# Attention scores: one VectorE instruction that masks, scales, moves and keeps the extreme, in place of mask matmuls, a reduction and a scaling

## The chip, the cores and the metric

One Trainium2 chip, one of its cores. The metric is the device time of one launch in microseconds. Before the change it was measured in three runs, with a median of 2131.19 us (2128.11 to 2140.74).

## What is computed

A sequence of two transformer-like layers on x of shape 2 x 1024 x 256 in float32: a Mamba-2 block with a gated MLP, a feed-forward block with weights from a lookup table, causal attention, and a mixture of experts. The change is in the attention alone:

```
q = einsum('bpd,hde->bphe', x, W_Q) + b_Q        # k and v in the same way
scores = einsum('bqhe,bkhe->bhqk', q, k) / sqrt(128)
scores = where(tril(ones((S, S))), scores, -100000.0)
attn = softmax(scores, axis=-1)
z = einsum('bkhe,bhqk->bqhe', v, attn)
out = einsum('bqhe,hed->bqd', z, W_O) + b_O      # S = 1024, 16 heads of 128, batch 2
```

## The kernel before

Matrix products of float32 precision are made of three passes over pairs (hi, lo): a value rounded to the matrix engine's fast float type and the rest. Every tensor that enters a product is therefore made twice: ACT writes hi from PSUM, DVE writes lo as the difference (L1597 to L1599 and L1642 to L1645).

Attention goes over 2 batches, and in each over 8 pairs of heads. An order of events is written out by hand in `section`, and each engine runs through the same list and picks its own part (`handle`). There are three kinds of section. "first" makes q, k and v of pair 0 and then the scores of its head 0 with nothing between them. "body" runs in a hardware loop, 7 turns per batch: it turns and sums the probabilities of one pair while it makes the scores of the next, the projections of the next pair, and the output of this one. "last" is a body without a next pair; it has the following norm in it.

A score tile t has 128 queries and (t+1) x 128 keys (t from 0 to 7), in two PSUM banks; tiles take turns with two such places. For a tile:

1. PE makes three passes for each chunk of up to 512 keys (L1525, L1529, L1530). In the chunk that ends on the diagonal it adds the causal mask with one more matmul, of a bf16 mask by a bf16 identity (L1528). Before it starts it waits until the exponential of tile t-2 is done (L1519), which frees the place.
2. DVE takes the negated maximum of the row (L1648), drains, and multiplies it by the scale (L1650).
3. ACT makes the exponential from PSUM into SBUF with that bias, and the row's sum (L1604; a second instruction reads the sum).
4. DVE takes the reciprocal of the sum (L1653), GpSimd multiplies the probabilities by it in place (L1692).
5. PE turns 128 x 128 blocks of the probabilities (L1538), ACT and DVE make the pair pt_hi, pt_lo of them, and PE sums with v (L1551 to L1559). The work banks 4 to 6 take turns; a sum waits for its own pt_lo, which is asked for two chunks ahead.
6. After the last chunk of a group ACT gathers z (L1612, L1614), DVE makes its lo (L1657), and PE multiplies it by W_O; DVE adds the output to x (L1661).

DVE's order in a chunk is: reciprocal of the tile before, maximum of this tile, pt_lo. ACT's is: pt_hi, gather, exponential, projection.

Of the kernel before, what the change touches and what calls it, by code (L numbers as in the profile page):

```python
# [7 lines left out]
BF16 = mybir.dt.bfloat16  # L8
# [6 lines left out]
P = 128  # L15
# [1231 lines left out]
def attention_stage(nc, sems, mem, s, a, before, norm):  # L1247
# [10 lines left out]
    def sb(what, shape, dt=F32):  # L1258
        return mem.enter_context(nc.sbuf_tensor(f"attn_{what}", shape, dt))
# [3 lines left out]

    q, k, v = pair("q", [P, 2, SEQ]), pair("k", [P, 2, SEQ]), pair("v", [P, QT, 2 * AE])
    z, pt = pair("z", [P, 2, SEQ]), pair("pt", [P, 3, GROUP])
    probs = [[sb(f"probs_{h}_{g}", [P, TG, (g + 1) * GROUP]) for g in range(2)] for h in range(2)]
    qkv_raw, wo_raw = sb("qkv_raw", [P, 3, KD, 2, AE]), sb("wo_raw", [P, 2, D])
    qkv, wo = pair("qkv", [P, 3, KD, 2, AE]), pair("wo", [P, 2, D])
    z_raw = sb("z_raw", [P, GROUP])
    bias = sb("bias", [P, 3, AH])  # L1270
    b_out = sb("b_out", [P, D])
    ident_b, mask = sb("ident_b", [P, P], BF16), sb("mask", [P, P], BF16)
    neg_max, sums, inverse = (sb(n, [P, 2 * QT]) for n in ("neg_max", "sums", "inverse"))

    small_loaded, qkv_loaded, wo_loaded, masks_ready = (
# [129 lines left out]
    def first_column(e):  # L1405

        return max(0, e["j"] - TG * e["g"]) * P

    def score_view(e):
        width = (e["t"] + 1) * P  # L1410
        slot = 2 * (e["t"] % 2)
        return s.psum[:, slot:slot + 2, :].rearrange("p b c -> p (b c)")[:, 0:width]

    def probs_view(e):
        return probs[e["h"]][e["t"] // TG][:, e["t"] % TG, 0:(e["t"] + 1) * P]

    def stat(tensor, e):
        at = e["h"] * QT + e["t"]
# [60 lines left out]

    def tensor(pe):  # L1480
        pe.wait_ge(*before)
        pe.wait_ge(masks_ready, 4)
        pe.sem_inc(summed, 3)

        def handle(e, counts, b, kind, i):
            what = e["what"]
            if what == "norm" and e["step"] == "turn":

                pe.wait_ge(exp_done, counts.at("tile", QT))
                norm["turn"](pe, norm_group(e, b))  # L1490
            if what in ("project", "values"):

# [21 lines left out]
            elif what == "score":  # L1514
# [1 line left out]
                pe.wait_ge(work_done, counts.at("work", e["need"]))  # L1516

                ahead = max(0, e["tile"] - 1) if kind == "first" else e["tile"] - 1
                pe.wait_ge(exp_done, counts.at("tile", ahead))  # L1519
                t, view = e["t"], score_view(e)  # L1520
                queries = pair_at(q, slice(None), e["h"], slice(t * P, (t + 1) * P))
                for at in range(0, (t + 1) * P, GROUP):
                    end = min(at + GROUP, (t + 1) * P)
                    (q_hi, q_lo), (k_hi, k_lo) = queries, pair_at(k, slice(None), e["h"], slice(at, end))
                    pe.matmul(view[:, at:end], q_hi, k_hi, start=True, stop=False)  # L1525
                    if end == (t + 1) * P:

                        pe.matmul(view[:, t * P:], ident_b[:, :], mask[:, :], start=False, stop=False)  # L1528
                    pe.matmul(view[:, at:end], q_hi, k_lo, start=False, stop=False)  # L1529
                    last = pe.matmul(view[:, at:end], q_lo, k_hi, start=False, stop=True)  # L1530
                last.then_inc(scores_ready, 1)
            elif what == "turn":

                tile = TG * (e["g"] + 1)
                ready = counts.at("tile", tile - QT) if e["h"] == 0 else counts.at("tile", tile)
                pe.wait_ge(probs_ready, ready)
                for lq in range(first_column(e) // P, TG):
                    last = pe.transpose(s.psum[:, work_bank(e), lq * P:(lq + 1) * P],  # L1538
                                        probs[e["h"]][e["g"]][:, lq, e["j"] * P:(e["j"] + 1) * P], s.ident[:, :])
                last.then_inc(work_ready, 1)  # L1540
            elif what == "sum":

                pe.wait_ge(work_done, counts.at("work", e["work"] + 1))
                j = e["j"]
                if j == 0:

                    pe.wait_ge(z_read, 1 + counts.at("z", 2 * e["h"] + e["g"]))
                at = first_column(e)
                v_hi, v_lo = pair_at(v, slice(None), j, slice(e["h"] * AE, (e["h"] + 1) * AE))
                p_hi, p_lo = pair_at(pt, slice(None), e["pt"] % 3)  # L1550
                pe.matmul(s.psum[:, 7, at:], v_hi, p_hi[:, at:], start=j == 0, stop=False, skip_group_check=True)  # L1551
                pe.matmul(s.psum[:, 7, at:], v_hi, p_lo[:, at:], start=False, stop=False, skip_group_check=True)  # L1552

                ends = at + P if j >= TG * e["g"] else at
                if ends > at:
                    last = pe.matmul(s.psum[:, 7, at:ends], v_lo, p_hi[:, at:ends], start=False, stop=True,
                                     skip_group_check=True)
                if ends < GROUP:
                    last = pe.matmul(s.psum[:, 7, ends:], v_lo, p_hi[:, ends:], start=False, stop=False, skip_group_check=True)  # L1559
                last.then_inc(summed, 1)  # L1560
            elif what == "output":

                pe.wait_ge(z_done, 1 + counts.at("z", 4))
                pe.wait_ge(w_split, counts.at("w", 1 if kind == "last" else 4))
                for t in range(2):
                    tokens = slice((2 * e["t"] + t) * P, (2 * e["t"] + t + 1) * P)
                    for h in range(2):
                        last = three_passes(pe, s.psum[:, work_bank(e), t * D:(t + 1) * D],
                                            pair_at(z, slice(None), h, tokens), pair_at(wo, slice(None), h), h == 0, h == 1)
                last.then_inc(work_ready, 1)  # L1570
# [3 lines left out]
    def scalar(act):  # L1574
# [4 lines left out]
        def handle(e, counts, b, kind, i):  # L1579
# [21 lines left out]
                norm["high"](act, norm_group(e, b))  # L1601
            elif what == "exp":
                act.wait_ge(max_ready, counts.at("tile", e["tile"] + 1))
                act.activation(probs_view(e), score_view(e), ACT.Exp, bias=stat(neg_max, e), scale=SCORE_SCALE,  # L1604
                               accum_out=stat(sums, e)).then_inc(exp_done, 1)
            elif what == "gather":

# [14 lines left out]
    def vector(dve):  # L1622
# [9 lines left out]
            dve.drain()  # L1632

        add_bias(0)

        def handle(e, counts, b, kind, i):
            what = e["what"]
# [7 lines left out]
                    dve.tensor_tensor(lo, work_view(e), hi.bitcast(F32), ALU.subtract).then_inc(work_done, 1)  # L1645
            elif what == "score":
                dve.wait_ge(scores_ready, counts.at("tile", e["tile"] + 1))
                dve.tensor_reduce(stat(neg_max, e), score_view(e), AX_X, ALU.max, negate=True)  # L1648
                dve.drain()
                dve.tensor_scalar(stat(neg_max, e), stat(neg_max, e), SCORE_SCALE, None, ALU.mult).then_inc(max_ready, 1)  # L1650
            elif what == "invert":
                dve.wait_ge(exp_done, counts.at("tile", e["tile"] + 1))
                dve.reciprocal(stat(inverse, e), stat(sums, e)).then_inc(inverse_ready, 1)  # L1653
# [16 lines left out]
    def gpsimd(pool):  # L1670

        pool.wait_ge(*before)
        pool.memset(ident_b[:, :], 0.0).then_inc(masks_ready, 1)
        pool.memset(mask[:, :], 0.0).then_inc(masks_ready, 1)
        pool.wait_ge(masks_ready, 2)
        pool.affine_select(out=ident_b[:, :], in_=ident_b[:, :], compare_op=ALU.not_equal, fill=1.0, base=0,
                           pattern=[[-1, P]], channel_multiplier=1).then_inc(masks_ready, 1)
        pool.affine_select(out=mask[:, :], in_=mask[:, :], compare_op=ALU.is_ge, fill=MASKED, base=0,
                           pattern=[[-1, P]], channel_multiplier=1).then_inc(masks_ready, 1)

        def handle(e, counts, b, kind, i):
# [652 lines left out]
```

## Time and profile before

| | us |
|---|---|
| median of 3 runs | 2131.19 |
| the profiled execution, its own time | 2131.62 |
| its span, first to last instruction | 2129.9 |
| attention, first to last of its matmuls | 718 to 1783 |

The profile is of one execution. A row of a group of instructions gives the line, engine, operation, output<-inputs, shapes and count, then the busy time in us and the mean of one in ns, then the engine's idle time before them and what ended it. A matmul's row is longer than the time by which it delays the next, since matmuls overlap: for PE the distance from start to start is the price. "granted clock" is the share of TensorE's full speed.

### The profile page before, as it was taken

Reading aid. Unit: us, or ns where it says so; the run is one execution under the profiler, and the core shown is the slowest. Engines: PE = TensorE matmul, PEld = TensorE weight load, DVE = VectorE, ACT = ScalarE, POOL = GpSimd, SP = SyncE. Lnnn points to the kernel's source line nnn. Section 1 sums busy time; section 2 is a strip of 40 time slices with the busy share of each in tenths; the row PEclk is TensorE's granted clock in tenths of the full one; section 3 lists DMA queues with packets and bytes.
Section 4 is the critical chain, followed back from the end, with each engine's and each line's share of the span. In section 5 each row is a group of like instructions: output and inputs, shape, how many; then the busy total and the mean of one; then the engine's idle time right before and its main releaser. Section 6 shows DMA issues by size and latency. Waiting matters only on the chain.

```text
span 2129.9 us, 34088 instructions
## 1 busy us (share of the span) xinstructions
PE 1897.3 (89%) x10870; PEld 1542.8 (72%) x10870; DVE 1400.8 (66%) x2757; ACT 972.2 (46%) x1984; POOL 638.8 (30%) x634
## 2 busy tenths in 40 slices
PE   2699889888999799999999989999999996999997
PEld 1455555577788578888888877888888885788886
DVE  6656362388865466666666656666666666688887
ACT  2333233255533265555655536555565553233332
POOL 5123234333333132222222213222222221234342
PEclk9789989799999899999999989999999998899999
DMA  3000001100000200000000000000000001000001
GB/s 95 1 1 1 1 1 40 50 15 12 5 1 1 39 21 20 20 20 0 20 20 5 16 20 21 20 20 19 1 20 20 5 1 45 16 16 30 15 0 40
DMA packets 59807, 37.71 MB, mean 18 GB/s; under 512 B 16488, under 2 KB 56656, under 8 KB 59728
## 3 DMA queue, kind: packets, MB, share of 16 engines
q1 hardware_dynamic: 59728, 36.71, 6.0%
q8 instruction: 44, 0.72, 0.1%
q14 instruction: 35, 0.29, 0.0%
HBM read 34.60 MB, written 2.10 MB: 17 GB/s over the span
## 4 chain that ended last, share of the span: by engine, by line
PE 71%; DVE 15%; ACT 5%; issue 4%; DVEq 3%; POOL 1%; DMA 0%; SPq 0%; ACTq 0%; POOLq 0%
PE psum L52 12%; PE psum L54 12%; PE psum L53 12%; PE psum L1538 6%; PE psum L1529 3%; PE psum L1525 3%; PE psum L1551 3%; PE psum L1530 3%; PE psum L1552 3%; PE psum L1559 3%; DVE mamba_conv_sum L1075 3%; PE psum L951 2%; PE psum L953 2%; DVE table_leaves L561 2%; ACT attn_probs L1604 1%
## 5 line engine op out<-in xcount | busy, mean ns | idle before, releaser
L1692 POOL TENSOR_SCALAR attn_probs<-attn_probs,attn_inverse 128x128 f32<-128x128 f32 (+7 forms) x256 | 191.0, 747 | 614.3 <-DVE attn_inverse L1653 614.1
L1599 ACT ACTIVATE attn_pt_hi<-psum 128x512 fp32r<-128x512 f32 (+3 forms) x384 | 185.6, 488 | 236.2 <-PE psum L1538 234.0
L1645 DVE TENSOR_TENSOR attn_pt_lo<-psum,attn_pt_hi 128x512 fp32r<-128x512 f32 (+3 forms) x384 | 211.4, 555 | 61.4 <-ACT attn_pt_hi L1599 58.0
L1604 ACT ACTIVATE attn_probs<-psum,attn_neg_max 128x128 f32<-128x128 f32 (+7 forms) x256 | 188.8, 737 | 118.8 <-DVE attn_neg_max L1650 118.4
L1538 PE MATMUL psum<-ident,attn_probs 128*128 128x128 f32 x1152 | 190.2, 276 | 27.7 <-DVE x_tok L1661 11.9
L1648 DVE TENSOR_REDUCE attn_neg_max<-psum 128x1 f32<-128x128 f32 (+7 forms) x256 | 192.0, 750 | 17.8 <-PE psum L1530 14.3
L1551 PE MATMUL psum<-attn_pt_hi,attn_v_hi 128*128 128x512 f32 (+3 forms) x384 | 162.3, 423 | 23.2 <-DVE attn_pt_lo L1645 17.6
L1538 PEld LDWEIGHTS psum<-ident,attn_probs 128*128 128x128 f32 x1152 | 137.6, 141 | 49.6 <-DVE attn_pt_lo L1645 18.6
L1529 PE MATMUL psum<-attn_k_lo,attn_q_hi 128*128 128x512 f32 (+3 forms) x384 | 151.9, 395 | 0.0
L1968 POOL TENSOR_TENSOR moe_hid_lo<-moe_hidden,moe_hid_hi 128x512 fp32r<-128x512 f32 x64 | 82.9, 1296 | 199.2 <-ACT moe_hid_hi L1941 199.2
L1525 PE MATMUL psum<-attn_k_hi,attn_q_hi 128*128 128x512 f32 (+3 forms) x384 | 136.7, 356 | 5.7 <-ACT attn_probs L1604 5.0
L1552 PE MATMUL psum<-attn_pt_lo,attn_v_hi 128*128 128x512 f32 (+3 forms) x384 | 134.8, 351 | 0.0
L1530 PE MATMUL psum<-attn_k_hi,attn_q_lo 128*128 128x512 f32 (+3 forms) x384 | 133.9, 349 | 0.0
L395 POOL TENSOR_TENSOR gated_h_lo<-gated_hidden,gated_h_hi 128x512 fp32r<-128x512 f32 x56 | 78.4, 1399 | 176.4 <-ACT gated_h_hi L383 176.4
L52 PE MATMUL psum<-act_hi,moe_gu_hi 128*128 128x512 f32 x256 | 105.9, 414 | 16.3 <-DVE moe_up L2041 13.1
L52 PE MATMUL psum<-act_hi,attn_qkv_hi 128*128 128x512 f32 x256 | 105.4, 412 | 15.8 <-POOL attn_qkv_lo L1685 15.8
L1559 PE MATMUL psum<-attn_pt_hi,attn_v_lo 128*128 128x512 f32 (+3 forms) x320 | 116.6, 364 | 0.0
L1685 POOL TENSOR_TENSOR attn_qkv_lo<-attn_qkv_raw,attn_qkv_hi 128x512 fp32r<-128x512 f32 x48 | 60.8, 1284 | 152.4 <-ACT attn_qkv_hi L1589 152.4
L53 PE MATMUL psum<-act_lo,moe_gu_hi 128*128 128x512 f32 x256 | 104.6, 409 | 0.0
L54 PE MATMUL psum<-act_hi,moe_gu_lo 128*128 128x512 f32 x256 | 104.2, 407 | 0.0
L54 PE MATMUL psum<-act_hi,attn_qkv_lo 128*128 128x512 f32 x256 | 103.0, 402 | 0.0
L53 PE MATMUL psum<-act_lo,attn_qkv_hi 128*128 128x512 f32 x256 | 102.4, 400 | 0.0
(322 smaller groups left out, 5479.2 us busy)
## 6 DMA issues: line engine op xcount, KB each, us to landing
attn_qkv_raw<-in_L_attn_W_Q_dram SPq DMA_DIRECT2D x32, 128.0 KB, 2.2
attn_qkv_raw<-in_L_attn_W_K_dram SPq DMA_DIRECT2D x32, 128.0 KB, 2.4
attn_qkv_raw<-in_L_attn_W_V_dram SPq DMA_DIRECT2D x32, 128.0 KB, 2.5
attn_wo_raw<-in_L_attn_W_O_dram SPq DMA_DIRECT2D x16, 256.0 KB, 3.0
moe_gu_raw<-_L_ffn_gate_up_proj_dram SPq DMA_DIRECT2D x8, 512.0 KB, 3.8
x_in<-_attn_hidden_states_dram SPq DMA_DIRECT2D x4, 512.0 KB, 5.6
x_tok<-_attn_hidden_states_dram SPq DMA_DIRECT2D x4, 512.0 KB, 5.9
moe_down_raw<-in_L_ffn_down_proj_dram SPq DMA_DIRECT2D x8, 256.0 KB, 4.1
```

The costliest lines, as they stand in the source:

```text
L52: pe.matmul(out, s_hi, m_hi, start=start, stop=False)
L53: pe.matmul(out, s_hi, m_lo, start=False, stop=False)
L54: return pe.matmul(out, s_lo, m_hi, start=False, stop=stop)
L1525: pe.matmul(view[:, at:end], q_hi, k_hi, start=True, stop=False)
L1529: pe.matmul(view[:, at:end], q_hi, k_lo, start=False, stop=False)
L1530: last = pe.matmul(view[:, at:end], q_lo, k_hi, start=False, stop=True)
L1538: last = pe.transpose(s.psum[:, work_bank(e), lq * P:(lq + 1) * P], probs[e["h"]][e["g"]][:, lq, e["j"] * P:(e["j"] + 1) * P], s.ident[:, :])
L1551: pe.matmul(s.psum[:, 7, at:], v_hi, p_hi[:, at:], start=j == 0, stop=False, skip_group_check=True)
L1552: pe.matmul(s.psum[:, 7, at:], v_hi, p_lo[:, at:], start=False, stop=False, skip_group_check=True)
L1604: act.activation(probs_view(e), score_view(e), ACT.Exp, bias=stat(neg_max, e), scale=SCORE_SCALE, accum_out=stat(sums, e)).then_inc(exp_do ...
L1645: dve.tensor_tensor(lo, work_view(e), hi.bitcast(F32), ALU.subtract).then_inc(work_done, 1)
L1648: dve.tensor_reduce(stat(neg_max, e), score_view(e), AX_X, ALU.max, negate=True)
```

## The change

The two bf16 constants and the mask matmul go. The mask becomes a float32 tile of 128 x 1024, zero but for its last 128 columns, whose part above the diagonal is -1e30. For each tile one DVE instruction (`tensor_tensor_reduce` with add and min) reads the scores from PSUM and the last (t+1) x 128 columns of the mask from SBUF, adds them, multiplies by minus the scale, writes the result to the probabilities' tile in SBUF, and keeps its minimum, which is the negated scaled maximum. The reduction, the drain and the scaling go. ACT's exponential reads and writes that SBUF tile in place, with scale -1. PE's scores, and the norm's transposes that use the same banks, wait for `max_ready` instead of `exp_done`. The probabilities of a head lie packed, row after row, where they were a rectangle for each half.

```
-    probs = [[sb(f"probs_{h}_{g}", [P, TG, (g + 1) * GROUP]) for g in range(2)] for h in range(2)]
+    probs = [sb(f"probs_{h}", [P, QT * (QT + 1) // 2 * P]) for h in range(2)]
-    ident_b, mask = sb("ident_b", [P, P], BF16), sb("mask", [P, P], BF16)
+    mask = sb("mask", [P, SEQ])
+    def row_start(t):
+        return t * (t + 1) // 2 * P
     def probs_view(e):
-        return probs[e["h"]][e["t"] // TG][:, e["t"] % TG, 0:(e["t"] + 1) * P]
+        return probs[e["h"]][:, row_start(e["t"]):row_start(e["t"] + 1)]
+    def probs_block(e, t):
+        at = row_start(t) + e["j"] * P
+        return probs[e["h"]][:, at:at + P]
...
     def tensor(pe):
-        pe.wait_ge(masks_ready, 4)
...
-                pe.wait_ge(exp_done, counts.at("tile", QT))
+                pe.wait_ge(max_ready, counts.at("tile", QT))
                 norm["turn"](pe, norm_group(e, b))
...
-                pe.wait_ge(exp_done, counts.at("tile", ahead))
+                pe.wait_ge(max_ready, counts.at("tile", ahead))
...
                     pe.matmul(view[:, at:end], q_hi, k_hi, start=True, stop=False)
-                    if end == (t + 1) * P:
-                        pe.matmul(view[:, t * P:], ident_b[:, :], mask[:, :], start=False, stop=False)
...
-                                        probs[e["h"]][e["g"]][:, lq, e["j"] * P:(e["j"] + 1) * P], s.ident[:, :])
+                                        probs_block(e, TG * e["g"] + lq), s.ident[:, :])
...
             elif what == "exp":
-                act.activation(probs_view(e), score_view(e), ACT.Exp, bias=stat(neg_max, e), scale=SCORE_SCALE,
+                act.activation(probs_view(e), probs_view(e), ACT.Exp, bias=stat(neg_max, e), scale=-1.0,
                                accum_out=stat(sums, e)).then_inc(exp_done, 1)
...
         add_bias(0)
+        dve.wait_ge(masks_ready, 2)
...
                 dve.wait_ge(scores_ready, counts.at("tile", e["tile"] + 1))
-                dve.tensor_reduce(stat(neg_max, e), score_view(e), AX_X, ALU.max, negate=True)
-                dve.drain()
-                dve.tensor_scalar(stat(neg_max, e), stat(neg_max, e), SCORE_SCALE, None, ALU.mult).then_inc(max_ready, 1)
+                dve.sem_inc(s.wait_over, 1)
+                dve.tensor_tensor_reduce(probs_view(e), score_view(e), mask[:, (QT - 1 - e["t"]) * P:], -SCORE_SCALE, -MASKED,
+                                         ALU.add, ALU.min, stat(neg_max, e)).then_inc(max_ready, 1)
...
     def gpsimd(pool):
-        pool.memset(ident_b[:, :], 0.0).then_inc(masks_ready, 1)
         pool.memset(mask[:, :], 0.0).then_inc(masks_ready, 1)
-        pool.wait_ge(masks_ready, 2)
-        pool.affine_select(out=ident_b[:, :], in_=ident_b[:, :], compare_op=ALU.not_equal, fill=1.0, base=0,
-                           pattern=[[-1, P]], channel_multiplier=1).then_inc(masks_ready, 1)
-        pool.affine_select(out=mask[:, :], in_=mask[:, :], compare_op=ALU.is_ge, fill=MASKED, base=0,
+        pool.wait_ge(masks_ready, 1)
+        pool.affine_select(out=mask[:, SEQ - P:], in_=mask[:, SEQ - P:], compare_op=ALU.is_ge, fill=MASKED, base=0,
                            pattern=[[-1, P]], channel_multiplier=1).then_inc(masks_ready, 1)
```

## Rows read from the trace of the kernel before

**Rows 1.** The page's head: span, and busy us (share) xinstructions of each engine.

```profile
span 2129.9 us, 34088 instructions
...
PE 1897.3 (89%) x10870; PEld 1542.8 (72%) x10870; DVE 1400.8 (66%) x2757; ACT 972.2 (46%) x1984; POOL 638.8 (30%) x634
```

**Rows 2.** Windows: stretch and length, busy us of each engine, granted clock, DMA.

```profile
737.60:754.40 16.80, 11.83 (x60) 8.12 (x59) 9.53 (x28) 8.60 (x21) 5.79 (x8) 0.90 0.00 0
...
880.50:943.80 63.30, 60.49 (x388) 52.21 (x388) 41.80 (x92) 37.55 (x80) 16.95 (x20) 1.00 0.06 17
```

**Rows 3.** Waits of PE in attention: us in total, times, longest us.

```profile
PE psum L1551 <- DVE attn_pt_lo L1645: 17.6, 21, 2.4
...
PE psum L1538 <- DVE x_tok L1661: 11.9, 14, 0.9
PE psum L1538 <- DVE attn_pt_lo L1645: 11.6, 13, 0.9
...
PE psum L1525 <- ACT attn_probs L1604: 5.0, 5, 1.5
```

**Rows 4.** Groups by line and shape.

```profile
L1528 PE MATMUL psum<-attn_mask,attn_ident_b 128*128 128x128 bf16 x256 | 59.4, 232 | 0.0
...
L1648 DVE TENSOR_REDUCE attn_neg_max<-psum 128x1 f32<-128x1024 f32 x32 | 38.9, 1215 | 0.6 <-PE psum L1530 0.6
...
L1648 DVE TENSOR_REDUCE attn_neg_max<-psum 128x1 f32<-128x128 f32 x32 | 9.1, 286 | 0.0
...
L1103 DVE TENSOR_TENSOR mamba_mixed<-mamba_decay,psum 128x1024 f32<-128x1024 f32 x16 | 19.5, 1222 | 14.1 <-ACT mamba_decay L1018 11.5 <-issue 2.6
...
L561 DVE COPY_PREDICATED table_leaves<-table_bits,table_leaves 128x512 f32<-128x512 uint8 x49 | 45.2, 954 | 3.2 <-issue 0.5
...
L1614 ACT ACTIVATE attn_z_hi<-attn_z_raw 128x512 fp32r<-128x512 f32 x64 | 40.5, 632 | 2.0
...
L1599 ACT ACTIVATE attn_pt_hi<-psum 128x512 fp32r<-128x512 f32 x192 | 114.5, 596 | 158.7 <-PE psum L1538 156.6
```

**Rows 5.** Timeline of PE in a body turn: start us, us, engine, line.

```profile
904.08 0.39 PE L1525 MATMUL psum<-attn_k_hi,attn_q_hi 128*128 128x512 f32 x1
...
904.76 0.39 PE L1525 MATMUL psum<-attn_k_hi,attn_q_hi 128*128 128x512 f32 x1
...
905.58 0.49 PE L1538 MATMUL psum<-ident,attn_probs 128*128 128x128 f32 x3
905.82 0.31 PE L1551 MATMUL psum<-attn_pt_hi,attn_v_hi 128*128 128x128 f32 x1
...
906.19 0.27 PE L1525 MATMUL psum<-attn_k_hi,attn_q_hi 128*128 128x128 f32 x1
...
906.60 0.41 PE L1538 MATMUL psum<-ident,attn_probs 128*128 128x128 f32 x2
```

**Rows 6.** Timeline of the same turn, the chain to PE's wait at 910.74.

```profile
907.21 0.15 DVE L1650 TENSOR_SCALAR attn_neg_max<-attn_neg_max 128x1 f32<-128x1 f32 x1
...
907.82 1.10 ACT L1604 ACTIVATE attn_probs<-psum,attn_neg_max 128x1024 f32<-128x1024 f32 x1
...
909.13 0.29 DVE L1648 TENSOR_REDUCE attn_neg_max<-psum 128x1 f32<-128x128 f32 x1
...
909.69 0.37 ACT L1604 ACTIVATE attn_probs<-psum,attn_neg_max 128x128 f32<-128x128 f32 x1 [0.41 <-DVE attn_neg_max L1650]
...
910.74 0.63 PE L1538 MATMUL psum<-ident,attn_probs 128*128 128x128 f32 x4 [0.94 <-DVE attn_pt_lo L1645]
```

**Rows 7.** Timeline of the first section of batch 0.

```profile
739.10 0.28 DVE L1648 TENSOR_REDUCE attn_neg_max<-psum 128x1 f32<-128x128 f32 x1
...
751.85 1.11 ACT L1604 ACTIVATE attn_probs<-psum,attn_neg_max 128x1024 f32<-128x1024 f32 x1 [0.79 <-DVE attn_neg_max L1650]
...
754.39 0.77 PE L1551 MATMUL psum<-attn_pt_hi,attn_v_hi 128*128 128x512 f32 x1 [2.42 <-DVE attn_pt_lo L1645]
```

**Rows 8.** Timeline of POOL at attention's start.

```profile
716.94 3.72 POOL L1685 TENSOR_TENSOR attn_qkv_lo<-attn_qkv_raw,attn_qkv_hi 128x512 fp32r<-128x512 f32 x3 [10.33 <-ACT attn_qkv_hi L1589]
```

## The prediction

> **What bounds the kernel now.** I read the busy shares first [rows 1]: the matrix engine is busy for 89% of the span, the vector engine for 66%, the activation engine for 46%. Such a mean hides stages, so next came the stages of attention alone [rows 2]. Attention runs from 718 to 1783 us. It holds two "first" sections (the row of 737.6 to 754.4 is the scores of one), fourteen body turns (seven per batch; the row of 880.5 to 943.8 is one, 63.3 us long) and two "last" sections. In a body turn PE is busy for 60.49 of 63.30 us at a granted clock of 1.00, with DVE at 41.80 and ACT at 37.55. So a body turn ends when PE has issued its stream: what leaves PE's stream is gained, what leaves DVE or ACT is gained only where PE waits for them. In a first section PE is busy for only 11.8 of 16.8 us; there nothing is interleaved with the scores, and the round trip PE, DVE, ACT sets the time.
>
> Third, what PE waits for in attention [rows 3]. The wait of L1538 for x_tok (14 times, 0.85 us) is an output tile and is untouched. The wait of L1538 for attn_pt_lo (13 times, 0.9 us) is one per body turn; its chain is in [rows 6]. The wait of L1525 for attn_probs (5.0 us in 5) is the scores waiting for the exponential of the tile two before, and lies in the first sections. The longest wait for attn_pt_lo, 2.4 us, stands at the end of a first section [rows 7].
>
> **The change part by part.**
>
> *Mask matmuls gone from PE (256).* The row of L1528 says 232 ns each, 59.4 us in all [rows 4], but matmuls overlap, so starts are what counts [rows 5]. Three passes over 512 columns without a mask matmul start at 904.08 and the next at 904.76: 0.68 us. The same three with one in between go from 904.76 to 905.58: 0.82 us. The mask costs 0.14, with width 512. At width 128, three passes of a sum without mask take 905.82 to 906.19, 0.37 us; scores with mask take 906.19 to 906.60, 0.41: only 0.04, since narrow passes wait for weights anyway. For widths 256 and 384 I have no clean pair here and take 0.13, near the 512 case. The last chunk of the eight tiles of a head has width 128 twice and a wider one six times: 2 x 0.04 + 6 x 0.13 = 0.86 us a head, 1.72 us a body turn. Not all of it shows: two 128-wide tiles and one 256-wide one lie just ahead of a wait that DVE or ACT ends (such as the one that ends at 910.74 [rows 6]); there PE would only wait longer. That leaves 1.72 - 0.08 - 0.13 = 1.51 us a turn, times 14 = 21.1 us. Bounds: 0.07 a mask on the exposed 13 (13 us in all), and 1.72 on each turn (24 us).
>
> *One fused DVE instruction for reduce, drain and 1-element scaling.* Before: 1215 ns at 1024 elements, 286 at 128, mean 750 [rows 4], then 0.15 us of L1650; at 909.13 the reduce begins and at 909.69 the exponential [rows 6]. The fused form is not in the trace. It reads PSUM and SBUF and writes SBUF, as L1103 does: 1222 ns at 1024. So streaming the scores out costs nothing over reducing them. The extreme has to be read out: a small instruction such as L1650 costs about 0.15 us [rows 6], of which I take half, 0.08, as seen. Taken: reduce's time plus 0.08, a saving of about 0.1 a tile. Bounds: below, the reduce alone (0.2 saved); above, the slowest two-input row, L561 at 954 ns for 512, 1.38 times a tensor_tensor of that width, plus a full 0.15: 1.8 us at 1024, 0.4 more than today's pair. In the body DVE has 21 us to spare a turn, so this matters only on the chain of [rows 6].
> The Trainium skill, VectorE: DVE Perf Modes, section "Two Vector instructions with no wait between them", says that an operation that also writes out its accumulator is two instructions; by it the read-out would have a row of its own, and the gain a tile would be near nothing. No run shown here tells.
>
> *The exponential reads SBUF instead of PSUM.* ACT's copy of 512 takes 632 ns from SBUF (L1614) and 596 from PSUM (L1599) [rows 4]: 0.04 us more, 256 times, 9 us of ACT, hidden under PE except twice on the chain of each turn.
> The Trainium skill on the same page, section "The TRN2 errata", gives 224 against 172 cycles, which would be an estimated 0.043 us; the rows agree.
>
> *The chain per body turn* [rows 6]: exponential of tile 7 (held up by the gather ahead of it on ACT, not by its maximum), its reciprocal, the maximum of tile 0, its exponential, pt_hi, pt_lo, PE at 910.74. New: -0.13 for the fused maximum (0.56 becomes 0.43), +0.04 for each of two exponentials: 0.05 less a turn. I count 0; bounds -2 and +3 us over 14 turns.
>
> *Score slots free earlier.* The scores of tile t wait for the maximum of t-2, not its exponential. In the body this wait hardly exists. In a first section it is the rhythm [rows 7]: the first reduce starts at 739.10, the exponential of tile 7 at 751.85, PE goes on at 754.39 after it. New: eight fused instructions, 8 x 0.75 + 8 x 0.08 = 6.6 us; seven reciprocals between them at 0.1, since DVE's order is maximum t, reciprocal t-1; and 0.6 in which DVE waits for scores of a still narrow tile: 7.9 us, last exponential at 747.1, 4.75 us sooner. PE needs twice 0.68 = 1.36 us for tile 7 without its mask [rows 5], about DVE's time, so it keeps up at full clock; but the clock granted in that stretch is 0.90 [rows 2], and I take off 0.75 for matmuls at the lower level. So 4.0 a section (2 to 5.5), 8 for both. Behind it the same order follows: what was late, PE's wait for pt_lo of chunk 0, stays and moves forward.
>
> *The last sections* hold eight scores each: 0.86 less 0.1 covered, 1.5 us for both (0 to 3).
>
> *Costed at nothing:* packed probabilities (same elements, all rows contiguous; transposes read 128-column blocks as before); PE's removed wait for the masks; DVE's new one, long met; GpSimd's mask of 1024 floats, made in the 10.33 us in which POOL waits for the first weights [rows 8]; if that cover were gone it would cost, once, less than the 3.72 us of the three subtractions of 512 behind it. DVE now writes the SBUF tile where ACT did, and nothing new is queued behind a wait.
>
> **Sum.** 21.1 + 0 + 8 + 1.5 = 30.6 us off the profiled execution's 2131.62 (its span is 2129.9): 2101. That execution lies 0.4 us above the median of 2131.19.
>
> **Rivals.**
> 1. *The fused instruction is slow per element*, two steps of 1.04 ns each instead of one (mean 576 elements: 0.6 us more). For it: no row shows the form. Against it: every two-input row at 512 lies between 689 and 954 ns. The body's slack takes most of it, since a sum waits for a pt_lo made two chunks earlier; but the maximum of tile 7 is 1.07 longer less the 0.15 of L1650, of which only the 0.46 from 907.36 to 907.82 are slack [rows 6], so the chain starts 0.46 late, and tile 0's is 0.13 longer: 0.59 x 14 = 8.3. A first section gains nothing (4.0 - 4.8). Sum: -21.1 + 8.3 + 1.6 - 1.5 = -12.7, 2119: within 1%.
> The Trainium skill, Vector Engine (DVE) Microarchitecture Reference, section "Points that are easy to get wrong", has a form of accumulating instruction halve its rate with two SBUF sources that are not bf16; here one source is PSUM, so by its words it would not apply, and nothing shown here tests it.
> 2. *Only the matmuls count*: the first sections stay, because PE runs them at the lower clock or the fused instruction lands at its upper bound. 2131.6 - 21.1 - 1 = 2110, the border of 1%.
> 3. *Slower: a fixed cost of the fused instruction*, x us whatever the width. It enters the chain of [rows 6] twice (once less about 0.5 of slack) and eight times in each first section: 14 x (2x - 0.5) + 16x = 44x - 7. It cancels the 30.6 at x = 0.85 us; at x = 1.3 the time is 2151. L1650's 0.15 us for one element speaks against it.
> 4. *More gained*: full clock in the first sections and the upper bound of the matmuls: 24 + 11 + 3 + 2 = 40, 2092.
>
> **How the numbers follow.** 1% of 2131, about what a measurement of this kernel can tell from no change, is 21 us: faster means under 2110. Chances: my forecast (2095 to 2108) 0.56, rival 4 0.10, rival 2 0.14 (half on each side of the border), rival 1 0.12, rival 3 0.08. Faster: 0.56 + 0.10 + 0.07 = 0.73; within 1%: 0.07 + 0.12 + 0.01 = 0.20; slower 0.07. The range goes from rival 4's 2092 to 2114, past rival 2; outside it lie rivals 1 and 3.
>
> **What would show it.** No L1528 rows, and body turns of 61.8 us instead of 63.3. Fused rows of about 1.22 to 1.3 us at 1024 and 0.29 to 0.37 at 128. First sections of 13 us. PE's L1525 waiting for DVE, briefly. The same two 0.86 us waits of PE a turn. It is wrong if the turn keeps 63 us (other waits took the mask's time), if the fused row at 1024 is over 2 us, or if PE waits for attn_pt_lo more than once or twice a turn.

## The result, and the profile after

| | before | after |
|---|---|---|
| median, us | 2135.41 (4 runs, 2128.11 to 2140.74) | 2103.19 (4 runs, 2100.11 to 2105.40) |
| profiled execution, us (its span) | 2131.62 (2129.9) | 2105.28 (2103.6) |

The ratio of the medians is 0.985, with a 95% interval from 0.982 to 0.988: 1.5% faster, 32 us by the medians and 26 us by the two profiled executions. The forecast was 2101, with the range 2092 to 2114.

The stages, marked in both traces by the same matmuls of PE (us):

| stage | before | after |
|---|---|---|
| first section, batch 0 / batch 1 | 16.73 / 16.64 | 12.83 / 12.83 |
| seven body turns, batch 0 / batch 1 | 442.45 / 444.87 | 432.04 / 431.98 |
| a typical body turn | 63.27 | 61.83 |
| last section up to its last score, batch 0 | 19.91 | 19.10 |
| rest of it, batch 0 | 34.81 | 36.89 |
| last section, batch 1 | 51.47 | 50.67 |
| everything ahead of attention's first projection | 718.35 | 722.24 |

First sections -7.7, body turns -23.3, last sections +0.5, the part ahead of attention +3.9, and +0.3 in the projections ahead of a batch's first scores and after attention: -26.3 together. The +3.9 isn't the change's: with the same code there, the kernels below have 717.4 to 721.9. Of the -23.3, 14 x 1.44 = 20.2 is the typical turn. The rest is the clock: four of before's fourteen turns hold a stretch at half speed, and two of after's (the first of each batch). Such a stretch makes a turn about 1.5 us longer, as two neighbouring turns of before show:

```profile
1475.80:1540.60 64.80, 62.12 (x390) 53.60 (x390) 41.86 (x92) 37.73 (x80) 16.96 (x20) 0.97 0.06 16
1540.60:1603.80 63.20, 60.52 (x390) 52.22 (x390) 41.81 (x92) 37.62 (x80) 16.96 (x20) 1.00 0.05 17
```

(stretch, length, busy us of PE, weight load, DVE, ACT, POOL, granted clock, DMA.)

The page's head of after, as [rows 1]:

```profile
span 2103.6 us, 33574 instructions
...
PE 1860.5 (88%) x10614; PEld 1537.1 (73%) x10614; DVE 1363.8 (65%) x2757; ACT 979.4 (47%) x1984; POOL 639.7 (30%) x632
```

Windows of after, as [rows 2] and with the same columns: the first section, a body turn (the fourth of batch 0, where [rows 2] has the third; they are alike), the rest of the last section of batch 0.

```profile
741.80:754.70 12.90, 8.85 (x51) 7.07 (x49) 8.48 (x28) 8.83 (x21) 5.84 (x8) 1.00 0.00 1
...
939.50:1001.30 61.80, 58.52 (x372) 52.10 (x372) 39.40 (x92) 38.03 (x80) 16.98 (x20) 1.00 0.06 17
...
1205.80:1242.70 36.90, 26.59 (x144) 23.31 (x142) 23.64 (x54) 14.39 (x27) 5.60 (x6) 0.77 0.00 1
```

The body turn has 1.97 us less of PE's work than [rows 2] and is 1.5 shorter: the difference went into waits.

What PE waits for in attention, as [rows 3]:

```profile
PE psum L1555 <- DVE attn_pt_lo L1650: 19.0, 20, 2.7
PE psum L1542 <- DVE attn_pt_lo L1650: 18.7, 14, 1.4
...
PE psum L1542 <- DVE x_tok L1666: 11.9, 14, 0.9
```

L1542 and L1555 are the old L1538 and L1551. The mid-turn wait for attn_pt_lo went from 0.9 to 1.3 us each time, 11.6 to 18.7 in all; the wait for x_tok is as it was; PE's wait for attn_probs in the scores has left the list.

Groups of after, as [rows 4]:

```profile
L1654 DVE CUSTOM_DVE_ANT_0 attn_probs<-psum,attn_mask 128x1024 f32<-128x1024 f32 x32 | 39.0, 1220 | 0.4 <-PE psum L1534 0.4
...
L1608 ACT ACTIVATE attn_probs<-attn_probs,attn_neg_max 128x128 f32<-128x128 f32 (+7 forms) x256 | 197.9, 773 | 99.1 <-DVE attn_neg_max L1654 98.8
...
L1654 DVE CUSTOM_DVE_ANT_0 attn_probs<-psum,attn_mask 128x128 f32<-128x128 f32 (+7 forms) x256 | 192.7, 753 | 17.1 <-PE psum L1534 9.0
```

The fused instruction takes 1220 ns at 1024 elements and 753 in the mean, where the bare reduction took 1215 and 750: adding the mask, scaling and writing a whole row back to SBUF cost nothing. What it saves stands in the timelines. Before, at 1024 elements, the reduction and then the scaling:

```profile
905.92 1.22 DVE L1648 TENSOR_REDUCE attn_neg_max<-psum 128x1 f32<-128x1024 f32 x1
907.21 0.15 DVE L1650 TENSOR_SCALAR attn_neg_max<-attn_neg_max 128x1 f32<-128x1 f32 x1
```

and after, the fused instruction and the read-out of its minimum, which lies inside the fused instruction's own time but for the last 0.01 us:

```profile
750.81 1.22 DVE L1654 CUSTOM_DVE_ANT_0 attn_probs<-psum,attn_mask 128x1024 f32<-128x1024 f32 x1 [0.22 <-PE psum L1534]
751.96 0.08 DVE L1654 DVE_READ_ACCUMULATOR2_ANT attn_neg_max<- 128x1 f32 x1
```

From the start of the one to the finished statistic it was 1.44 us and is 1.23. In the mean of all 256 tiles it was 0.98 and is 0.76: 0.22 saved a tile.

### The profile page after: what moved, and what is told of

Its sections match the earlier page's. It is cut to its first block, busy times and chain, and to the rows that moved or that the text cites. A ratio compares the mean times of both kernels' runs of the same rounds, so it can differ in the third digit from the quotient of the medians.

```text
span 2103.6 us, 33574 instructions
## 1 busy us (share of the span) xinstructions
PE 1860.5 (88%) x10614; PEld 1537.1 (73%) x10614; DVE 1363.8 (65%) x2757; ACT 979.4 (47%) x1984; POOL 639.7 (30%) x632
## 4 chain that ended last, share of the span: by engine, by line
PE 72%; DVE 14%; ACT 5%; issue 4%; DVEq 3%; POOL 1%; DMA 0%; SPq 0%; ACTq 0%; POOLq 0%
PE psum L52 13%; PE psum L53 12%; PE psum L54 12%; PE psum L1542 6%; PE psum L1555 3%; PE psum L1532 3%; PE psum L1534 3%; PE psum L1533 3%; PE psum L1556 3%; PE psum L1563 3%; DVE mamba_conv_sum L1075 3%; PE psum L951 2%; PE psum L953 2%; DVE table_leaves L561 2%; PE psum L942 1%
## 5 line engine op out<-in xcount | busy, mean ns | idle before, releaser
L1608 ACT ACTIVATE attn_probs<-attn_probs,attn_neg_max 128x128 f32<-128x128 f32 (+7 forms) x256 | 197.9, 773 | 99.1 <-DVE attn_neg_max L1654 98.8
L1542 PE MATMUL psum<-ident,attn_probs 128*128 128x128 f32 x1152 | 190.4, 277 | 33.9 <-DVE attn_pt_lo L1650 18.7
L1654 DVE CUSTOM_DVE_ANT_0 attn_probs<-psum,attn_mask 128x128 f32<-128x128 f32 (+7 forms) x256 | 192.7, 753 | 17.1 <-PE psum L1534 9.0
L1555 PE MATMUL psum<-attn_pt_hi,attn_v_hi 128*128 128x512 f32 (+3 forms) x384 | 161.3, 420 | 25.8 <-DVE attn_pt_lo L1650 19.0
L1542 PEld LDWEIGHTS psum<-ident,attn_probs 128*128 128x128 f32 x1152 | 137.9, 142 | 56.1 <-DVE attn_pt_lo L1650 24.8
L1533 PE MATMUL psum<-attn_k_lo,attn_q_hi 128*128 128x512 f32 (+3 forms) x384 | 132.6, 345 | 0.0
```

Source lines behind the costliest of these rows:

```text
L1608: act.activation(probs_view(e), probs_view(e), ACT.Exp, bias=stat(neg_max, e), scale=-1.0, accum_out=stat(sums, e)).then_inc(exp_done, 1)
L1654: dve.tensor_tensor_reduce(probs_view(e), score_view(e), mask[:, (QT - 1 - e["t"]) * P:], -SCORE_SCALE, -MASKED, ALU.add, ALU.min, stat(ne ...
```

## The experiments

All but e4 start from the changed kernel. A turn is a typical body turn, from trace marks; "first" is the mean of both first sections.

| kernel | median, us | ratio to before (95%) | turn | first |
|---|---|---|---|---|
| before | 2134 to 2135 | 1 | 63.27 | 16.7 |
| after | 2103.19 | 0.985 (0.982 to 0.988) | 61.83 | 12.8 |
| e1, mask matmuls back | 2128.07 | 0.998 (0.996 to 0.999) | 63.26 | 13.3 |
| e2, scores wait for the exponential | 2105.27 | 0.987 (0.985 to 0.990) | 61.80 | 15.2 |
| e3, fused instruction twice | 2274.59 | 1.067 (1.065 to 1.070) | 72.1 to 73.7 | 17.9 |
| e4, before without mask matmuls | 2114.19 | 0.991 (0.989 to 0.994) | 61.8 | 16.2 |
| e5, 0.6 us of DVE work on every tile | 2184.38 (one run) | | 65.4 to 68.3 | 15.6 |
| e6, the same work on tile 0 only | 2105.89 (one run) | | 61.83 | 14.1 |
| e7, z_hi and z_lo a chunk later | 2101.08 | 0.984 (0.982 to 0.986) | 61.27 | 12.8 |
| e9b, output banks dealt | 2092.13 | 0.981 (0.978 to 0.983) | 61.07 | 12.8 |
| e10, e9b and an earlier projection | 2086.82 | 0.978 (0.976 to 0.980) | 60.77 | 12.8 |
| e11b, e10 and e7 | 2094.41 | 0.981 (0.979 to 0.984) | 60.77 | 12.8 |

**Which part of the change pays: e1, e2, e4.**

e1 puts the mask matmul back and keeps all else:

```
+                    if end == (t + 1) * P:
+                        pe.matmul(view[:, t * P:], ident_b[:, :], mask_b[:, :], start=False, stop=False)
```

> The new kernel with the 256 bf16 mask matmuls put back between the three passes (the fused instruction masks as well, so the mask is added twice). Theory A, the matmuls themselves make the shorter body turn: a turn goes from 61.83 us back to 63.2 to 63.4, the first sections (first score to first sum, 12.83 us) grow by under 1 us each, the whole is 21 to 24 us slower than the changed kernel. Rival B, the turn is shorter because the chain through the maximum is: a turn stays under 62.5 us, the whole under +10.

e2 puts back the scores' wait:

```
-                pe.wait_ge(max_ready, counts.at("tile", ahead))
+                pe.wait_ge(exp_done, counts.at("tile", ahead))
```

> The new kernel, but PE's scores wait for the exponential of tile t-2 (exp_done) again instead of its fused maximum. Theory A, the first sections are shorter because the place is free earlier: 16.0 to 16.7 us each instead of 12.83, body turns stay at 61.8, the whole +6 to +8 us against the changed kernel. Rival, they are shorter because one instruction took the place of two on DVE: 14 us or less each, the whole +3 at most.

e4 is the kernel before with the mask matmul's two lines taken out:

> The kernel before, with the mask matmuls left out and all else as it was (so the attention is not causal within the diagonal blocks). Theory A: body turns of 61.8 to 62.0 us with the old reduce, drain and scaling, first sections of 16.0 to 16.7 us, the whole 20 to 24 us under the kernel before and 6 to 9 over the changed one. Rival B: turns of 63 us or more.

The body turn follows the mask matmuls alone: 63.26 with them whatever DVE does (e1), 61.8 without them, with the old reduction, drain and scaling (e4) or with the new instruction (after). So the body's 1.44 us a turn is theirs. The first section splits less cleanly. Before 16.7; without mask matmuls alone 16.2 (e4): 0.5, which e1 against after shows again (13.3 and 12.8). With the fused instruction too, but the scores waiting for the exponential, 15.15 (e2): 1.05. With the earlier release of the slots 12.8: 2.3. That last term is the largest, and e2 and after differ in it alone, both at a granted clock of 1.00. The 1.05 is not the instruction's for certain: before and e4 ran their first sections at a clock of 0.90 and 0.89, e2 at 1.00, and the clock can be worth as much. e6, of which more below, has one first section at either clock, with the same code:

```profile
740.20:753.60 13.40, 8.79 (x50) 6.95 (x48) 8.96 (x31) 8.76 (x21) 5.79 (x8) 1.00 0.00 0
1257.40:1272.10 14.70, 10.27 (x50) 7.99 (x49) 8.95 (x31) 8.78 (x21) 5.81 (x8) 0.88 0.00 0
```

The instruction saves eight times 0.22 us there, the lower clock cost 1.3; the two are not told apart. Nor do the runs tell why the clock stays full early in the first sections of every kernel with the fused instruction, but for one section each of e3 and e6.

What missed its forecast: e1 is 24.9 us over after by the medians (21 to 24 expected), and in its profiled execution four turns besides the first of each batch hold a stretch at half speed, where after has none. e4 lies 11.0 over after (6 to 9 expected). e2's 15.15 lies between its theory (16.0 to 16.7) and its rival (14 or less), and e2 costs only 2 us by the medians against 4.6 by its first sections: the rest of its last section of batch 0 is 2.1 shorter than after's. The intervals of e2 and after overlap, so the total doesn't prove the release's worth; the stage does.

**What a DVE microsecond costs in the body: e3, e5, e6.**

e3 issues the fused instruction twice for each tile, with a drain between:

```
+                dve.tensor_tensor_reduce(probs_view(e), score_view(e), mask[:, (QT - 1 - e["t"]) * P:], -SCORE_SCALE, -MASKED,
+                                         ALU.add, ALU.min, stat(neg_max, e))
+                dve.drain()
```

> The new kernel with each fused instruction issued twice, with a drain between: 0.37 us more on DVE for tile 0 and 1.30 for tile 7 of each head, 0.83 on average, 13 us a body turn. Theory A, a body turn has one chain through DVE and slack elsewhere: a turn grows by 0.37 for tile 0 and about 0.7 for tile 7 (1.30 less 0.6 of slack), to about 62.9 us; a first section by 5 to 6 us; the whole +26 against the changed kernel. Rival C, DVE is close to the bound everywhere: a turn grows by 4 us or more, the whole by 60 or more.

e5 puts three additions of 128 x 128 ahead of each fused instruction, results unused; e6 the same, under `if e["t"] == 0`:

```
+                for n in range(3):
+                    dve.tensor_tensor(filler[:, 3 * (e["t"] % 2) + n, :], score_view(e)[:, 0:P], mask[:, 0:P], ALU.add)
```

> The new kernel with three 128-column additions on DVE (0.29 us a row, about 0.75 together) ahead of each fused instruction, its results unused. Theory of the prediction, one chain per turn through the maxima and slack elsewhere: a body turn grows by 2 x 0.75 less 0.5, 1.0 us, to 62.8; first sections by 6 us. Theory D, which the doubled instruction points to: DVE's slack is used up where wide tiles follow each other, although it is idle a third of the time: the turn grows by 4 us or more.

> The same three additions, but ahead of the fused instruction of tile 0 of each head alone. If the maximum of tile 0 is on the chain that ends PE's long wait in mid-turn (as the prediction has it, by way of pt_lo), a turn grows by about 0.7 us to 62.5. If that wait is ended by GpSimd's scaling of tile 7 instead, which depends on nothing of tile 0, the turn stays within 0.2 us of 61.83.

The three additions turned out shorter than the 0.75 us that both expectations took: from the start of the first to the start of the fused instruction it is 0.60 us, at every tile of e5 and e6. Together they added 48.24 - 39.40 = 8.8 us of DVE to a turn whose mean slack was 22, and the turns grew by 5.0 us in the mean; e3's grew by 10.8. Theory D and rival C held. Windows of e5 (columns as above): a turn, then 20 us in its middle.

```profile
952.30:1019.50 67.20, 62.60 (x372) 54.89 (x372) 48.24 (x140) 37.27 (x80) 17.05 (x20) 0.95 0.05 16
...
972.30:977.30 5.00, 4.97 (x29) 4.21 (x28) 2.77 (x9) 2.58 (x7) 0.92 (x1) 1.00 0.00 0
977.30:982.30 5.00, 3.70 (x22) 2.93 (x21) 4.39 (x12) 3.98 (x8) 1.02 (x1) 0.94 0.00 0
982.30:987.30 5.00, 4.29 (x19) 3.92 (x19) 3.92 (x19) 1.74 (x6) 1.97 (x3) 0.50 0.00 0
987.30:992.30 5.00, 5.00 (x27) 4.24 (x26) 3.41 (x9) 3.76 (x8) 0.45 (x1) 0.88 0.00 0
```

And what PE waits for in that turn (us, times, longest):

```profile
PE psum L1556 <- DVE attn_pt_lo L1651: 1.6, 2, 0.9
PE psum L1543 <- DVE x_tok L1669: 0.9, 1, 0.9
PE psum L52 <- DVE attn_v_lo L1651: 0.9, 1, 0.9
PE psum L1543 <- POOL attn_probs L1697: 0.7, 1, 0.7
```

Of the 5.4 us by which this turn is longer than after's, 1.3 are waits (PE idle 4.6 against 3.3 us) and 4.1 are PE's own busy time (62.6 against 58.5, same matmuls). DVE was busy for 4.39 of the 5 us from 977.3, PE for only 3.70 (it waited 0.38 and 0.90 us), and right behind it the granted clock is 0.50, half speed, that is 1.2 GHz, with 0.88 after it. In after, PE waits 0.37 and then 1.34 us in the same place, and the clock stays:

```profile
964.50:969.50 5.00, 3.29 (x24) 2.77 (x23) 3.67 (x12) 3.60 (x9) 1.49 (x2) 1.00 0.00 0
969.50:974.50 5.00, 5.00 (x33) 4.34 (x32) 2.99 (x7) 4.51 (x10) 0.48 (x1) 1.00 0.00 0
```

So it does in the next turn of e5, although PE waits there for 0.37, 0.91 and 1.21 us, more than in the turn above. The whole turn (65.4 us), then the two windows with the waits and the one behind them:

```profile
1019.50:1085.00 65.50, 59.87 (x373) 52.39 (x373) 48.16 (x140) 36.98 (x80) 17.02 (x20) 1.00 0.05 16
1044.60:1049.60 5.00, 3.67 (x24) 2.84 (x22) 4.40 (x11) 3.96 (x8) 1.02 (x1) 1.00 0.00 0
1049.60:1054.60 5.00, 3.79 (x26) 3.36 (x26) 4.70 (x21) 3.33 (x9) 1.97 (x3) 1.00 0.00 0
1054.60:1059.60 5.00, 5.00 (x31) 4.34 (x30) 4.27 (x11) 3.31 (x8) 0.59 (x1) 1.00 0.00 0
```

That turn is 3.6 us longer than after's at full clock: 2.3 of waits and 1.3 of PE's busy time. Two of e5's fourteen turns are like it. The other twelve hold one to three stretches at half speed and take 66.5 to 68.3 us. So of the 5.0 us in the mean most is there without the clock, and about 1.4 come with it. e3 shows both at a larger size: in one of its turns PE is idle for 8.97 us (5.7 more) and busy for 64.59 (6.1 more) at a clock of 0.93, and every turn of e3 has such stretches. The Trainium skill's TensorE: Matmul & The Clock Gate, section "A second HAM failure mode: psum-queue depth-cycling", tells of a kernel whose PE idles briefly and often between groups of matmuls, and loses throughput to a clock that goes back and forth between its two levels; e3's and e5's rows agree in kind. But e5's two turns at full clock show that waits of this size do not bring the lower clock each time, and I ran nothing that lowers the clock without adding waits, so cause and effect stay open.

e6 adds its 0.6 us on tile 0 alone, on the chain that the prediction took for the one that ends the mid-turn wait. The turn doesn't move, nor does the wait (1.34 us). Only its label does:

```profile
965.00 1.12 POOL L1698 TENSOR_SCALAR attn_probs<-attn_probs,attn_inverse 128x1024 f32<-128x1024 f32 x1 [3.83 <-DVE attn_inverse L1662]
965.45 0.28 DVE L1658 CUSTOM_DVE_ANT_0 attn_probs<-psum,attn_mask 128x128 f32<-128x128 f32 x1
...
966.27 0.63 PE L1543 MATMUL psum<-ident,attn_probs 128*128 128x128 f32 x4 [1.34 <-POOL attn_probs L1698]
...
966.46 0.29 DVE L1651 TENSOR_TENSOR attn_pt_lo<-psum,attn_pt_hi 128x128 fp32r<-128x128 f32 x1
```

(timeline of e6: start, us, engine, line; in brackets the idle time before it and what ended it.) PE goes on at 966.27, before that pt_lo has even begun, and 0.15 us after GpSimd's scaling of tile 7 ends at 965.00 + 1.12. The same chain in after:

```profile
965.45 0.63 ACT L1618 ACTIVATE attn_z_hi<-attn_z_raw 128x512 fp32r<-128x512 f32 x1
...
965.98 1.14 ACT L1608 ACTIVATE attn_probs<-attn_probs,attn_neg_max 128x1024 f32<-128x1024 f32 x1
...
967.24 0.16 DVE L1658 RECIPROCAL attn_inverse<-attn_sums 128x1 f32<-128x1 f32 x1 [0.44 <-ACT attn_probs L1608]
...
967.49 0.29 DVE L1654 CUSTOM_DVE_ANT_0 attn_probs<-psum,attn_mask 128x128 f32<-128x128 f32 x1
967.61 1.54 POOL L1694 TENSOR_SCALAR attn_probs<-attn_probs,attn_inverse 128x1024 f32<-128x1024 f32 x2 [3.82 <-DVE attn_inverse L1658]
967.71 0.08 DVE L1654 DVE_READ_ACCUMULATOR2_ANT attn_neg_max<- 128x1 f32 x1
...
968.51 0.29 DVE L1650 TENSOR_TENSOR attn_pt_lo<-psum,attn_pt_hi 128x128 fp32r<-128x128 f32 x1
...
968.87 0.63 PE L1542 MATMUL psum<-ident,attn_probs 128*128 128x128 f32 x4 [1.34 <-DVE attn_pt_lo L1650]
```

GpSimd's scaling (by e6's row 1.12 us for tile 7, from 967.61, so 968.73; the row above holds two) and pt_lo (968.80) end within 0.1 us of each other just before PE's 968.87; the trace names the later. A wait for several semaphores is put down to whichever came last, and that misled me here.

**Shortening the chain that does decide: e7, e9b, e10, e11b.**

e7 makes z_hi and z_lo an event of their own, queued one chunk behind their gather, so that ACT comes to the exponential of tile 7 sooner:

```
+                if gathered:
+                    events.append(dict(gathered, what="zsplit"))
+                    gathered = None
...
-                    add("gather", ("z",), h=h, g=g)
+                    gathered = add("gather", ("z",), h=h, g=g)
...
```

> The new kernel, with the second half of the gather (z_hi on ACT, 0.63 us, and z_lo on DVE) moved one chunk later, so that the exponential of tile 7 comes right after z_raw. If the chain of the mid-turn wait goes z_raw, exponential of tile 7, reciprocal, scaling by GpSimd, PE: 0.5 us less a turn, to 61.3, 7 to 8 us less in all against the changed kernel. If it goes through tile 0 and pt_lo: the exponential of tile 0 now has z_hi ahead of it instead, and the turn stays at 61.8.

The turn falls to 61.27, and the timeline of e7 has PE's wait at 0.80 us in place of 1.34, ended by the same scaling:

```profile
960.48 1.12 POOL L1701 TENSOR_SCALAR attn_probs<-attn_probs,attn_inverse 128x1024 f32<-128x1024 f32 x1 [3.26 <-DVE attn_inverse L1665]
...
961.74 0.63 PE L1548 MATMUL psum<-ident,attn_probs 128*128 128x128 f32 x4 [0.80 <-POOL attn_probs L1701]
```

With e6 this settles it: mid-turn PE waits for z_raw, z_hi, exponential of tile 7, reciprocal, GpSimd. At 0.56 us a turn that is 7.8 us, but the total hardly moves (2101.08 against 2103.19; 7 to 8 were expected). In the profiled execution two more turns than in after have a stretch at half speed, which leaves 4.6 us of gain in the body, and the last sections took more than that back (38.90 us against 36.89 for the rest of batch 0's, 56.66 against 50.67 for batch 1's).

e9b lets the four output tiles of a group write the banks 5, 4, 5, 6 and relaxes the waits to match:

```
+        if e["what"] == "output":
+            return (5, 4, 5, 6)[e["t"]]
```

> The changed kernel with one further edit: the output tiles of a group take the banks 5, 4, 5, 6 in turn, so that none follows the other on the bank that was written last, and the scores' wait is relaxed to match. My theory: the wait of PE for x_tok, 0.86 us once a body turn (14 turns), is the output tile waiting for its bank, and goes; the body turn falls from 61.8 to 61.0 to 61.2 us and the kernel is 9 to 12 us under the changed one's 2103. Rival: PE's wait moves to the next wait of the turn, which grows by as much, and the turn stays at 61.8.

The wait for x_tok is gone and the turn is 61.07, 0.76 less; 14 x 0.76 = 10.6 of the 11.1 us by which the median fell.

e10 adds to that an earlier first projection of a turn's second half:

```
-                if c % half in project_at and not last:
-                    project(h)[project_at.index(c % half)]()
+                places = (1, 6, 8, 10) if h == 1 else project_at
+                if c % half in places and not last:
+                    project(h)[places.index(c % half)]()
```

> The new kernel with PE's two longest waits of a turn filled: in the second half the first projection comes two chunks earlier (after chunk 1 instead of 3), where PE waits 1.34 us; and the work banks of the four output tiles are dealt so that the next turn's first transposes need not wait for the last output (0.86 us). Nothing is computed differently. If waits and not the stream bound these places, the turn is 61.8 - 1.3 - 0.6 = 59.9 us, the whole 25 to 28 us under the changed kernel. Rival, another wait takes their place: 61 us or more, under 10 us gained.

The turn went to 60.77 only, between the forecast and its rival: the 1.34 us wait is filled, and a wait of 0.87 for z_raw appears behind it. What PE waits for in e10's attention:

```profile
PE psum L1563 <- DVE attn_pt_lo L1658: 20.2, 21, 2.7
PE psum L1563 <- ACT attn_z_raw L1624: 18.8, 30, 0.9
```

In after the second row was 6.7 us in 16. e10 is the fastest kernel of this study, 0.978 of before and 16 us under after.

e11b joins e7 and e10:

> The changed kernel with three further edits: the dealt output banks, the first projection of the second half earlier, and the lo part of a group's z (z_hi, z_lo) made one chunk after its gather, as its own event. With the first two alone the turn was 60.77 us and the kernel 2086.8. My theory: the wait that is left in mid-turn (0.87 us, for z_raw, after the projection was moved) and the chain z_raw, z_hi, exponential of tile 7, GpSimd's scaling are both on ACT's order, so that taking z_hi out of that chain gives another 0.4 to 0.6 us a turn: 60.2 to 60.4 us, 2079 to 2081 in all. Rival: the chain no longer decides once the projection fills it, and the turn stays at 60.8.

The rival held: the turn stays at 60.77, since the wait for z_raw is ACT's gather itself, which e7's edit doesn't move. And the kernel is 7.6 us slower than e10. Of the 9.6 us between the two profiled executions 7.7 lie in the last sections (rest of batch 0's: 37.41 against 34.20; batch 1's: 55.11 against 50.63). The rest of batch 0's in e10, then in e11b:

```profile
1196.15:1230.35 34.20, 22.17 (x144) 19.44 (x142) 23.42 (x54) 14.20 (x27) 5.58 (x6) 0.90 0.00 1
```

```profile
1196.71:1234.12 37.41, 26.12 (x143) 22.96 (x142) 24.27 (x54) 14.41 (x27) 5.57 (x6) 0.77 0.00 1
```

The rows of PE's waits there agree to 0.1 us for every row but one (L209 behind issue, 2.6 and 1.9 us). What differs is the clock, 0.90 against 0.77, and with it the time that nearly the same matmuls keep PE busy. Why a shift of z_hi by one chunk brings a lower clock into the last sections stays open.

## Why the prediction was right, point by point

The total came out near 2101 in part by luck. Against the profiled execution before, the body gained 23.3 us where 21.1 was forecast (3.1 of them by the clock), the first sections 7.7 where 8 was, and all the rest, where a gain of 1.5 was, took back 4.7, most of it ahead of attention, where nothing was changed: 26 in place of 30.6. The medians differ by 32: before's is 3.8 us above its profiled execution, after's 2.1 below its own.

- **Mask matmuls, 1.51 us a turn.** Measured 1.44, and e4 shows that it is theirs alone. Two of its terms were off against each other: the turn's PE time fell by 1.44 plus 0.56 of new idle time (2.73 to 3.29 us), 2.0 in all, so a mask cost 0.125 us in the mean and not the 0.108 of the sum; and what the waits covered was 0.56, not 0.21.
- **The fused instruction, reduce's time plus 0.08, a saving of about 0.1.** The rate was right (1220 and 286 ns), the saving was not: 0.22 us a tile, at the bound that the prediction gave for no read-out at all. The read-out has a row of its own (83 ns in the mean), but it ends with the fused instruction, so it adds 0.01 and not 0.08; and the old pair took longer than its two rows, 1.44 us against 1.22 + 0.15 at 1024. The sentence of the Trainium skill that the prediction cites (VectorE: DVE Perf Modes, "Two Vector instructions with no wait between them") holds: the accumulator's read-out is an instruction of its own. That the gain would be near nothing was my reading of it, and was wrong; the body hides the gain (e4 and after both 61.8).
- **The exponential from SBUF, 0.04.** Measured 773 against 737 ns in the mean: 0.036, hidden.
- **The chain per body turn, counted 0.** The sum of it was right, the chain was not. The prediction had PE's mid-turn wait end with tile 0: maximum, exponential, pt_hi, pt_lo. It ends with GpSimd's scaling of tile 7 (e6, e7), a path which has no fused instruction behind the exponential. So the -0.13 of the fused maximum was never on it, and the +0.04 of one exponential, not two, was. The trace named pt_lo because both paths end together, within 0.1 us.
- **"DVE has 21 us to spare a turn".** This is the step that failed, though the result didn't hang on it. By it, e5's 16 x 0.6 us and e3's 16 second instructions should have cost about a microsecond a turn; they cost 5.0 and 10.8. The spare time is a mean. Where wide maxima meet the pt_lo or v_lo that PE asks for next, e5's DVE is 88% busy (4.39 of 5 us), and PE waits there; the lower clock comes on top in most turns. So rival 1 (8.3 us lost in the body by 0.6 us more a tile) and rival 3 (44x - 7) were priced far too low: e5 added just that much, though the same to each tile and not in proportion to its width, and its body is 70 us longer. If the loss grew evenly with the added time (an estimate from e5's 81 us in all), a fixed cost of 0.22 to 0.23 us would have cancelled the forecast gain, and not one of 0.85. Neither rival came about, because the instruction runs at the reduction's rate; the 2151 of rival 3 was no bound of a slower outcome.
- **First sections, 4.0 each.** Measured 3.9 and 3.8, at the 13 us that was named, again with errors that cancel. DVE waited for scores for 1.9 us (0.39, 0.60, 0.18, 0.51 and 0.22), not 0.6, and its instructions took 0.4 less than counted: from its first maximum to the last exponential it took 8.8 us, not 7.9. But the 0.75 taken off for a low clock wasn't due: the granted clock in that stretch was 1.00, where before had 0.90, and nothing here shows that the change brought that about. The first and the last steps:

```profile
743.26 0.28 DVE L1654 CUSTOM_DVE_ANT_0 attn_probs<-psum,attn_mask 128x128 f32<-128x128 f32 x1
...
752.07 1.15 ACT L1608 ACTIVATE attn_probs<-attn_probs,attn_neg_max 128x1024 f32<-128x1024 f32 x1 [0.39 <-DVE attn_neg_max L1654]
...
754.65 0.49 PE L1555 MATMUL psum<-attn_pt_hi,attn_v_hi 128*128 128x512 f32 x1 [2.74 <-DVE attn_pt_lo L1650]
```

  Against [rows 7] the exponential starts 3.9 us sooner after the first maximum, and PE's wait for pt_lo at the end stayed and moved forward (2.42, now 2.74), as written.
- **Last sections, 1.5 for both.** The part with the scores fell by 0.8, the whole of batch 1's by 0.8: 1.6. The rest of batch 0's grew by 2.1 at a clock of 0.77 against 0.80 (e2 and e4 have 34.8 there, as before has). This is the one term of the result that no step foresaw.
- **PE's two waits of 0.86 a turn "the same".** Wrong for one of them: 0.94 ([rows 6]) became 1.34. Work that leaves PE ahead of a wait which another engine ends is not gained; I had counted three of sixteen masks as covered, and by the idle time it was four to five (0.56 / 0.125).

## What to carry to other kernels

Price work on an engine that isn't the bottleneck at the places where the bottleneck waits for it, not by its mean slack over a stage: here 0.6 us on each of 16 tiles cost 5 us a turn, with 22 us of mean slack. Where two paths end within 0.1 us of a wait, the trace's name for it is a coin toss: lengthen one of them by a known amount and see whether the wait moves. Compare stages at the same granted clock before you put a difference down to the code. And once an engine's stream is shortened, look for the waits that grew: here dealing the banks and moving a projection were worth another 16 us, half of what the change had given.

## What the runs showed of the hardware

- A fused add, scale, store and minimum over a PSUM row and an SBUF row runs at the speed of a bare reduction: 1220 against 1215 ns at 1024 elements, 286 against 286 at 128. The read-out of its minimum has a row of 83 ns, but ends 0.01 us after the fused instruction; against a reduction and a scaling with a drain between them the statistic is ready 0.22 us sooner.
- Work on an engine with much mean slack can cost about half its length: 8.8 us more of DVE in a turn of e5 (mean slack 22 us) made it 3.6 us longer at full clock and 5.0 in the mean.
- A stretch at half speed costs a body turn about 1.5 us, in before (63.2 and 64.8 us) as in after (61.8 and 63.4). Waits alone don't foretell it: the clock stayed at 1.00 through waits of 0.37, 0.91 and 1.21 us in one turn of e5, and fell to 0.50 behind 0.38 and 0.90 us in another.
- The end of attention ran at two clocks, 0.90 in e10 and 0.77 in e11b and after, with nearly the same matmuls and waits. e10's and e11b's totals stay apart over four runs each: 2082.4 to 2088.9 and 2093.1 to 2095.3.
